# Cross attention on one Trainium2 core: row maxima by products in row tiles, other slots, and keys split by GpSimd

## The chip, the cores and the metric

One core of a Trainium2 chip runs the whole program in one launch. The metric is device time in microseconds. The engines are TensorE (PE in the rows, its weight loads PEld), VectorE (DVE), ScalarE (ACT), GpSimd (POOL) and SyncE (SP, which here issues all DMAs).

## The reference, cut to what matters

A decoder layer on x of 16 batches x 56 tokens x 128: token and channel attention, cross attention to 1500 context rows per batch, and a mixture of eight experts. The change lies in the cross attention, with 16 heads of depth 8:

```python
q = _split_heads(query @ wq.T + bq, B)      # 16, 16, 56, 8
k = _split_heads(value @ wk.T + bk, B)      # 16, 16, 1500, 8
v = _split_heads(value @ wv.T + bv, B)
scores = jnp.einsum('bhqd,bhkd->bhqk', q, k) / scale
attn = jax.nn.softmax(scores, axis=-1)
ctx = jnp.einsum('bhqk,bhkd->bhqd', attn, v)
```

## The kernel before

Three stages follow each other: the token and channel attention (to about 114 us), the cross attention (to about 523 us), and the experts. Each is a block with one instruction stream per engine; semaphores order them.

**Keys.** For each batch, `project_keys` (L203) makes the keys in three chunks of 500, head dimension on partitions, in PSUM. ScalarE reads each chunk twice in `read_keys` (L225): rounded to fp32r as `k_hi` (L234), then whole as `k_full` (L235), which frees the bank. GpSimd makes `k_lo` = `k_full` - `k_hi` in `split_keys` (L237, L244). Keys of batch 0 are made within the first stage (L412, L468, L735), those of batch 1 at the opening of the cross attention (L968, L1008, L1139), all others in the loop. Around both openings GpSimd also computes the reciprocal roots for a layer norm (L146, L148), VectorE applies them to eight tiles of 128 columns in `normed` (L122, L124), and in the first stage GpSimd then sets `values` to 1 (L413). SyncE copies `k_hi`, `k_lo` and `k_hi` again into `k_stack` (L918), so that one product of 97 rows gives the scores with their low parts and the negated maximum as a row.

**Maximum.** Before the scores of a batch, each query row's maximum is estimated from the high parts alone. The 896 rows (16 heads x 56 tokens) are seven tiles of 128. `q_block_hi` holds the queries of each row at the 8 partitions of its own head and zeros elsewhere (L973), so one product of 128 x 128 by 128 x 500 (`max_scores`, L1158 to L1172) gives a tile's scores for a chunk; 7 x 3 = 21 products per batch, each into a bank of its own. VectorE reduces each (`take_max`, L1072) into `chunk_max`, joins the chunks of tiles 0 to 3 and 4 to 6 (`join_max`, L1081); TensorE turns the result (`turn_max`, L1181), ScalarE negates it (L1018), and SyncE brings the rows to `q_stack` by seven DMAs (`load_shift`, L934).

**Order.** All engines walk through periods of one batch with 12 slots (KT), one per tile of 125 keys. A slot t begins with `scores` (L1183, four products of 97 rows, S below); ScalarE takes their exponentials (L1024). Four tiles at once are weighed with the values (`weigh`, L1201, 32 products of fp32, two passes each, W below) in WEIGH_SLOTS, on column tiles of 32. The sums are copied (L1030), the denominators made (L1220), inverted (L1094), the heads scaled (L1098) and projected (L1227, 56 columns) in the period after. Keys for batch b + 2, values for b + 1 and the two turns for b + 1 have slots of their own. MAX_PLACES says how many maximum products follow in each slot: right behind the scores, ahead of W, behind W. Those from slot EARLY on belong to batch b + 2, the others to b + 1. Key, value, output, turn and maximum results take the banks 4, 5 and 7 in turn (`bank_turns`); a use waits until the third use before it has been read (`take_bank`, L1153). Before the loop all 21 maxima of batch 0 and eight (AHEAD) of batch 1 are made.

Of the kernel before, what the change touches and what calls it, by code (L numbers as in the profile page):

```python
# [9 lines left out]
ALU = mybir.AluOpType  # L10
# [14 lines left out]
HALF = HQ // 2  # L25
# [55 lines left out]
def build(nc, x_in, ctx_in, mats_in, rows_in, cols_in, gate_in, consts_in, const_at, wgu_in, wd_in, out):  # L81
    ctx = ExitStack()
    with ctx:
# [85 lines left out]
        def later(n, first):  # L169
            return not isinstance(n, int) or n >= first  # L170
# [54 lines left out]
        def read_keys(act, b, j, u, c, bank=MISC):  # L225

            if later(b, 1):
                act.wait_ge(k_lo_ready, KC * (b - 1) + c + 1)
            act.wait_ge(k_projected, KC * b + c + 1)
            k = slice(KW * c, KW * c + KW)  # L230
            if c == 0 and later(b, 2):
                act.wait_ge(stack_loaded[j], 16 * STACK_DMAS * u)
                act.wait_ge(max_scored, QT7 * KC * (b - 1))
            nc.scalar.activation(k_hi[:, j, k], bank[:, 0:KW], ACT.Identity, bias=COL["bk"]).then_inc(k_hi_ready, 1)  # L234
            nc.scalar.activation(k_full[:, k], bank[:, 0:KW], ACT.Identity, bias=COL["bk"]).then_inc(k_ready, 1)  # L235

        def split_keys(pool, b, j, u):  # L237

            if later(b, 2):
                pool.wait_ge(stack_loaded[j], 16 * STACK_DMAS * u)  # L240
            for c in range(KC):
                pool.wait_ge(k_ready, KC * b + c + 1)
                k = slice(KW * c, KW * c + KW)
                nc.gpsimd.tensor_tensor(k_lo[:, j, k], k_full[:, k], k_hi[:, j, k].bitcast(F32), ALU.subtract  # L244
                                        ).then_inc(k_lo_ready, 1)
# [560 lines left out]
        with s2:  # L806


            EARLY = 8
            MAX_PLACES = [(2, 0, 2), (0, 0, 0), (1, 2, 0), (1, 0, 0), (0, 1, 0), (1, 0, 1),  # L810
                          (1, 0, 0), (1, 0, 0), (1, 0, 0), (2, 1, 1), (0, 0, 1), (0, 1, 1)]
            KEY_SLOTS, VALUE_SLOTS, TURN_SLOTS = [2, 3, 4], [1, 6, 7], [3, 8]
            SUMS_SLOT, DEN_SLOT, INVERT_SLOTS, SCALE_SLOT, OUT_SLOT = 1, 2, [3, 4], 4, 8
            RING, QUAD, WEIGH_SLOTS = 6, 4, [0, 5, 9]
            HALF_TILES = [slice(0, -(-HALF // 128)), slice(-(-HALF // 128), QT7)]
            HALF_ROWS = HALF_TILES[0].stop
            TURNING_BANKS = [4, 5, 7]
# [36 lines left out]
            def max_bank(b, n):  # L854
                return BANK_OF["max", n] if later(b, 1) else (n + 4) % 6
# [49 lines left out]
            with nc.Block() as block:  # L905

                @block.sync
                def _(sp):
# [21 lines left out]
                    def load_shift(b, j, a):  # L930

                        sp.wait_ge(rows_ready, 2 * b + a + 1)
                        for r, t in enumerate(range(HALF_TILES[a].start, HALF_TILES[a].stop)):
                            sp.dma_start(q_stack[SHIFT_ROW:SHIFT_ROW + 1, j, 128 * t:128 * t + 128].bitcast(F32),  # L934
                                         neg_rows[r:r + 1, j, a, :].bitcast(F32)).then_inc(shift_loaded[j], 16)
# [114 lines left out]
                def _(dve):  # L1050
# [18 lines left out]
                    def take_max(b, j, n):  # L1069

                        dve.wait_ge(max_scored, QT7 * KC * b + n + 1)
                        nc.vector.tensor_reduce(out=chunk_max[:, n // KC, n % KC:n % KC + 1],  # L1072
# [64 lines left out]
                def _(pe):  # L1137
# [20 lines left out]
                    def max_scores(b, j, n):  # L1158
# [3 lines left out]
                        if n < KC:  # L1162
                            pe.wait_ge(k_hi_ready, KC * b + n + 1)
# [4 lines left out]
                        elif n >= 6:  # L1168
                            pe.wait_ge(max_taken, n - 5)
                        t, c = n // KC, n % KC  # L1170
                        nc.tensor.matmul(PS[:, max_bank(b, n), 0:KW], q_block_hi[:, j, 128 * t:128 * t + 128],  # L1171
                                         k_hi[:, j, KW * c:KW * c + KW], start=True, stop=True).then_inc(max_scored, 1)  # L1172
# [449 lines left out]
```

## Time and profile before

| | us |
|---|---|
| three runs | 668.26, 673.27, 677.43; median 673.27 |
| profiled execution | 676.67, its span 674.9 |
| cross attention, from the scores of batch 1 to those of batch 14 | 173.44 to 478.29 of the span |
| mean granted clock of TensorE | 0.944 |

Times in the rows are microseconds from the span's start unless marked ns. An instruction's busy time runs from its start to its end; matmuls are pipelined, so the ends of one overlap with the starts of the next, and the distance from start to start tells what one costs the engine.

### The profile page before, as it was taken

What the parts mean: (1) busy time and instruction counts of PE and PEld (TensorE: products, weight loads), DVE (VectorE), ACT (ScalarE), POOL (GpSimd) and SP (SyncE); (2) the same over time, 40 slices, a digit from 0 to 9 for tenths busy, and PEclk for the clock granted to TensorE, in tenths of its full rate; (3) what the DMA queues carried; (4) which work ended last, traced back from release to release, by engine and by line L of the source; (5) the groups of instructions that cost most, each with busy time, mean ns of one, the idle gap of its engine ahead of it and who ended that gap; (6) DMA issues with size and microseconds to landing.
All of it is one profiled execution on the core that took longest, in us unless ns stands there. A gap on an engine that the chain in (4) does not pass through costs nothing. (4 is left out here: it accounts for less than half of the span.)

```text
span 674.9 us, 17191 instructions
## 1 busy us (share of the span) xinstructions
PE 601.8 (89%) x6538; PEld 488.5 (72%) x6538; DVE 449.3 (67%) x806; ACT 338.1 (50%) x522; POOL 179.1 (27%) x143
## 2 busy tenths in 40 slices
PE   3799376679999999999999999999987489999997
PEld 1566165337787778778777877877776379999997
DVE  5764775887777878787887787787822464444443
ACT  2467344207656756665675576566554253333321
POOL 2673601422322423232242324123000211121100
PEclk9799888669999999999999999999989589999999
DMA  5000001575745663674467366536620011111100
GB/s 207 1 2 2 0 1 37 114 157 106 177 111 121 137 156 94 137 160 121 107 137 168 99 141 139 131 97 139 133 100 2 10 50 48 47 47 47 47 17 29
DMA packets 26221, 60.33 MB, mean 89 GB/s; under 512 B 14408, under 2 KB 15304, under 8 KB 26184
## 3 DMA queue, kind: packets, MB, share of 16 engines
q1 hardware_dynamic: 26184, 59.82, 36.4%
q8 instruction: 25, 0.41, 0.3%
q14 instruction: 12, 0.10, 0.0%
HBM read 20.53 MB, written 0.46 MB: 31 GB/s over the span
## 5 line engine op out<-in xcount | busy, mean ns | idle before, releaser
L1072 DVE TENSOR_REDUCE chunk_max<-PS 128x1 f32<-128x500 f32 x336 | 214.2, 674 | 58.6 <-PE PS L1171 56.8
L1024 ACT ACTIVATE P<-PS 125x896 f32<-125x896 f32 x192 | 173.6, 914 | 122.2 <-PE PS L1195 121.3
L1171 PE MATMUL PS<-k_hi,q_block_hi 128*128 128x500 f32 x336 | 132.5, 449 | 8.2 <-ACT k_full L235 3.4
L1195 PE MATMUL PS<-q_stack,k_stack 97*125 97x224 f32 x768 | 122.2, 282 | 2.7 <-ACT P L1024 2.5
L1195 PEld LDWEIGHTS PS<-q_stack,k_stack 97*125 97x125 f32 x768 | 106.8, 190 | 17.9 <-issue 6.8
L1171 PEld LDWEIGHTS PS<-k_hi,q_block_hi 128*128 128x128 f32 x336 | 62.3, 197 | 39.9 <-ACT k_full L235 16.8
L244 POOL TENSOR_TENSOR k_lo<-k_full,k_hi 128x500 fp32r<-128x500 f32 x48 | 60.3, 1258 | 103.7 <-ACT k_full L235 103.7
L1513 DVE TENSOR_TENSOR hidden<-gated,PS 128x448 f32<-128x448 f32 x64 | 39.7, 621 | 70.0 <-PE PS L1570 63.6
L1211 PE MATMUL PS<-P,values 125*32 125x112 f32 x3072 | 85.2, 263 | 0.6 <-ACT P L1024 0.5
L1211 PEld LDWEIGHTS PS<-P,values 125*32 125x32 f32 x3072 | 73.3, 111 | 13.9 <-issue 10.4
L1425 ACT ACTIVATE gated<-PS 128x448 f32<-128x448 f32 x64 | 34.9, 546 | 81.3 <-PE PS L1570 76.7
L982 POOL TENSOR_TENSOR q_stack<-q_copies,consts 96x896 fp32r<-96x896 f32 x16 | 26.8, 1677 | 143.6 <-PE PS L1195 131.4
L1548 PEld LDWEIGHTS PS<-w_down,hidden 128*128 128x128 f32 x448 | 57.6, 191 | 1.5
L1548 PE MATMUL PS<-w_down,hidden 128*128 128x128 f32 x448 | 57.9, 274 | 0.0
L206 PE MATMUL PS<-ctxT,mats 128*128 128x500 f32 x96 | 48.7, 589 | 7.1 <-ACT k_full L235 5.5
L1568 PE MATMUL PS<-T_hi,w_hi 128*128 128x448 f32 x128 | 52.5, 410 | 1.8 <-DVE hidden L1513 1.8
L214 PE MATMUL PS<-mats,ctxT 128*125 128x128 f32 x384 | 49.7, 273 | 0.0
L214 PEld LDWEIGHTS PS<-mats,ctxT 128*125 128x125 f32 x384 | 48.0, 188 | 1.3 <-issue 0.2
L1570 PE MATMUL PS<-T_hi,w_lo 128*128 128x448 f32 x128 | 47.7, 373 | 0.0
L1569 PE MATMUL PS<-T_lo,w_hi 128*128 128x448 f32 x128 | 47.7, 373 | 0.0
L234 ACT ACTIVATE k_hi<-PS,cols 128x500 fp32r<-128x500 f32 x48 | 32.3, 672 | 24.5 <-PE PS L206 23.2
L1390 POOL TENSOR_TENSOR w_lo<-w_gate_up,w_hi 128x1024 fp32r<-128x1024 f32 x8 | 19.0, 2376 | 92.2 <-ACT w_hi L1409 92.2
(139 smaller groups left out, 698.1 us busy)
## 6 DMA issues: line engine op xcount, KB each, us to landing
k_stack<-k_hi SPq DMA_DIRECT2D x128, 187.5 KB, 4.6
ctxT<-ctx_in SPq DMA_DIRECT2D x16, 750.0 KB, 4.3
k_stack<-k_lo SPq DMA_DIRECT2D x64, 187.5 KB, 4.5
w_gate_up<-wgu_in SPq DMA_DIRECT2D x8, 512.0 KB, 4.1
w_down<-wd_in SPq DMA_DIRECT2D x8, 256.0 KB, 2.8
q_stack<-neg_rows SPq DMA_DIRECT2D x112, 0.5 KB, 1.9
q_copies<-q_hi SPq DMA_DIRECT2D x8, 112.0 KB, 2.6
mats<-mats_in SPq DMA_DIRECT2D x1, 832.0 KB, 5.5
```

The source lines that it names most:

```text
L206: nc.tensor.matmul(bank[:, 0:KW], MAT["wk"], ctxT[:, j, KW * c:KW * c + KW], start=True, stop=True).then_inc(k_projected, 1)
L214: last = nc.tensor.matmul(bank[0:KR, 128 * t:128 * t + 128], ctxT[:, j, k0:k0 + KR], MAT["wv"], start=True, stop=True)
L244: nc.gpsimd.tensor_tensor(k_lo[:, j, k], k_full[:, k], k_hi[:, j, k].bitcast(F32), ALU.subtract).then_inc(k_lo_ready, 1)
L1024: nc.scalar.activation(P[:, t % RING, :].rearrange("p (a n) -> p a n", a=2), PS[0:KR, 2 * (t % 2):2 * (t % 2) + 2, 0:HALF], ACT.Exp).then_ ...
L1072: nc.vector.tensor_reduce(out=chunk_max[:, n // KC, n % KC:n % KC + 1], in_=PS[:, max_bank(b, n), 0:KW], axis=AX.X, op=ALU.max).then_inc(m ...
L1171: nc.tensor.matmul(PS[:, max_bank(b, n), 0:KW], q_block_hi[:, j, 128 * t:128 * t + 128], k_hi[:, j, KW * c:KW * c + KW], start=True, stop= ...
L1195: last = nc.tensor.matmul(PS[0:KR, 2 * (t % 2) + g // 2, o:o + GH * N], k_stack[:, j, g, KR * t:KR * t + KR], q_stack[0:SHIFT_ROW + 1, j, ...
L1211: last = nc.tensor.matmul(PS[32 * k:32 * k + 32, 6, 2 * N * r:2 * N * r + 2 * N], values[:, j, t, g, :], P[:, t % RING, 2 * N * g:2 * N * ...
L1548: last = nc.tensor.matmul(PS[:, 4 + 2 * j + p // 4, 128 * (p % 4):128 * (p % 4) + 128], hidden[:, j, t, 128 * p:128 * p + 128], w_down[:, ...
L1568: nc.tensor.matmul(bank, w_hi[:, j, w], hi, start=True, stop=False)
L1569: nc.tensor.matmul(bank, w_hi[:, j, w], lo, start=False, stop=False)
L1570: nc.tensor.matmul(bank, w_lo[:, j, w], hi, start=False, stop=True).then_inc(done, 1)
```

## The change

1. Each of the seven row tiles of queries touches only certain heads, so its product reads only the partitions (TILE_ROWS) where `q_block_hi` isn't zero: 32 rows for tiles 0, 2, 4 and 6, each in another quarter of the array, 64 for tiles 1 and 5, all 128 for tile 3. The results are the same sums. The order is by place (TILE_ORDER) and, within the groups of places, by chunk (MAX_ORDER): four products of 32 rows for each chunk, then two of 64 for each chunk, then three full ones. A chunk of keys is first waited for at products 0, 4 and 8.
2. EARLY, MAX_PLACES and all slots are new; three products per chunk group may follow each other in one place.
3. ScalarE reads a chunk of keys once, into `k_full`. GpSimd multiplies it by 1 into `k_hi` (fp32r, rounded), waits for that, and subtracts as before. The wait on `max_scored` moves to GpSimd.

```diff
--- before.py
+++ after.py
@@ -228,19 +228,19 @@
                 act.wait_ge(k_lo_ready, KC * (b - 1) + c + 1)
             act.wait_ge(k_projected, KC * b + c + 1)
             k = slice(KW * c, KW * c + KW)
-            if c == 0 and later(b, 2):
-                act.wait_ge(stack_loaded[j], 16 * STACK_DMAS * u)
-                act.wait_ge(max_scored, QT7 * KC * (b - 1))
-            nc.scalar.activation(k_hi[:, j, k], bank[:, 0:KW], ACT.Identity, bias=COL["bk"]).then_inc(k_hi_ready, 1)
             nc.scalar.activation(k_full[:, k], bank[:, 0:KW], ACT.Identity, bias=COL["bk"]).then_inc(k_ready, 1)
 
         def split_keys(pool, b, j, u):
 
             if later(b, 2):
                 pool.wait_ge(stack_loaded[j], 16 * STACK_DMAS * u)
+                pool.wait_ge(max_scored, QT7 * KC * (b - 1))
             for c in range(KC):
                 pool.wait_ge(k_ready, KC * b + c + 1)
                 k = slice(KW * c, KW * c + KW)
+                nc.gpsimd.tensor_tensor(k_hi[:, j, k], k_full[:, k], C["ones"][:, 0:1].broadcast_to([128, KW]), ALU.mult
+                                        ).then_inc(k_hi_ready, 1)
+                pool.wait_ge(k_hi_ready, KC * b + c + 1)
                 nc.gpsimd.tensor_tensor(k_lo[:, j, k], k_full[:, k], k_hi[:, j, k].bitcast(F32), ALU.subtract
                                         ).then_inc(k_lo_ready, 1)
 
@@ -806,14 +806,19 @@
         with s2:
 
 
-            EARLY = 8
-            MAX_PLACES = [(2, 0, 2), (0, 0, 0), (1, 2, 0), (1, 0, 0), (0, 1, 0), (1, 0, 1),
-                          (1, 0, 0), (1, 0, 0), (1, 0, 0), (2, 1, 1), (0, 0, 1), (0, 1, 1)]
-            KEY_SLOTS, VALUE_SLOTS, TURN_SLOTS = [2, 3, 4], [1, 6, 7], [3, 8]
-            SUMS_SLOT, DEN_SLOT, INVERT_SLOTS, SCALE_SLOT, OUT_SLOT = 1, 2, [3, 4], 4, 8
-            RING, QUAD, WEIGH_SLOTS = 6, 4, [0, 5, 9]
-            HALF_TILES = [slice(0, -(-HALF // 128)), slice(-(-HALF // 128), QT7)]
+            EARLY = 9
+            MAX_PLACES = [(1, 0, 3), (0, 0, 0), (0, 0, 0), (0, 0, 2), (0, 0, 0), (0, 2, 2), (0, 1, 0), (0, 1, 0), (1, 0, 0), (1, 0, 0), (2, 1, 2), (2, 0, 0)]
+            KEY_SLOTS, VALUE_SLOTS, TURN_SLOTS = [2, 4, 6], [2, 5, 8], [4, 9]
+            SUMS_SLOT, DEN_SLOT, INVERT_SLOTS, SCALE_SLOT, OUT_SLOT = 0, 1, [1, 4], 6, 9
+            RING, QUAD, WEIGH_SLOTS = 6, 4, [0, 5, 10]
+            TILE_ROWS = [(0, 32), (0, 64), (32, 64), (0, 128), (64, 96), (64, 128), (96, 128)]
+            TILE_ORDER = [0, 2, 4, 6, 1, 5, 3]
+            HALF_TILES = [slice(0, 4), slice(4, 7)]
             HALF_ROWS = HALF_TILES[0].stop
+            MAX_ORDER = ([(place, c) for c in range(KC) for place in range(0, 4)]
+                         + [(place, c) for c in range(KC) for place in range(4, 6)]
+                         + [(6, c) for c in range(KC)])
+            FIRST_OF_CHUNK = {MAX_ORDER.index((0, c)): c for c in range(KC)}
             TURNING_BANKS = [4, 5, 7]
             assert sum(map(sum, MAX_PLACES)) == QT7 * KC
             AHEAD = sum(map(sum, MAX_PLACES[EARLY:]))
@@ -930,7 +935,7 @@
                     def load_shift(b, j, a):
 
                         sp.wait_ge(rows_ready, 2 * b + a + 1)
-                        for r, t in enumerate(range(HALF_TILES[a].start, HALF_TILES[a].stop)):
+                        for r, t in enumerate(TILE_ORDER[HALF_TILES[a]]):
                             sp.dma_start(q_stack[SHIFT_ROW:SHIFT_ROW + 1, j, 128 * t:128 * t + 128].bitcast(F32),
                                          neg_rows[r:r + 1, j, a, :].bitcast(F32)).then_inc(shift_loaded[j], 16)
 
@@ -1069,7 +1074,7 @@
                     def take_max(b, j, n):
 
                         dve.wait_ge(max_scored, QT7 * KC * b + n + 1)
-                        nc.vector.tensor_reduce(out=chunk_max[:, n // KC, n % KC:n % KC + 1],
+                        nc.vector.tensor_reduce(out=chunk_max[:, MAX_ORDER[n][0], MAX_ORDER[n][1]:MAX_ORDER[n][1] + 1],
                                                 in_=PS[:, max_bank(b, n), 0:KW], axis=AX.X, op=ALU.max
                                                 ).then_inc(max_taken, 1)
 
@@ -1159,17 +1164,19 @@
 
                         if n == 0:
                             pe.wait_ge(q_blocks, b + 1)
-                        if n < KC:
-                            pe.wait_ge(k_hi_ready, KC * b + n + 1)
+                        if n in FIRST_OF_CHUNK:
+                            pe.wait_ge(k_hi_ready, KC * b + FIRST_OF_CHUNK[n] + 1)
                         if later(b, 1):
                             take_bank(max_bank(b, n), (max_taken, QT7 * KC * b + n + 1))
                         elif n == 4:
                             pe.wait_ge(q_split, 2)
                         elif n >= 6:
                             pe.wait_ge(max_taken, n - 5)
-                        t, c = n // KC, n % KC
-                        nc.tensor.matmul(PS[:, max_bank(b, n), 0:KW], q_block_hi[:, j, 128 * t:128 * t + 128],
-                                         k_hi[:, j, KW * c:KW * c + KW], start=True, stop=True).then_inc(max_scored, 1)
+                        place, c = MAX_ORDER[n]
+                        t = TILE_ORDER[place]
+                        r = slice(*TILE_ROWS[t])
+                        nc.tensor.matmul(PS[:, max_bank(b, n), 0:KW], q_block_hi[r, j, 128 * t:128 * t + 128],
+                                         k_hi[r, j, KW * c:KW * c + KW], start=True, stop=True).then_inc(max_scored, 1)
 
                     def turn_max(b, a):
 
```

## Rows read from the trace of the kernel before

The timeline views have: start, us busy, engine, line, operation, output<-inputs, shapes, count, and in brackets the idle time before and what ended it.

**Rows 1.** Windows view, 13 periods: length, busy of PE, PEld, DVE, ACT, POOL, granted clock.

```profile
173.44:478.29 304.85, 301.81 (x3939) 242.07 (x3940) 244.49 (x391) 193.06 (x274) 92.17 (x66) 1.00 0.56 129
```

**Rows 2.** Timeline of VectorE in one period.

```profile
312.70 3.78 DVE L1072 TENSOR_REDUCE chunk_max<-PS 128x1 f32<-128x500 f32 x6 [0.70 <-PE PS L1171]
```

**Rows 3.** Timeline of TensorE, parts of one period.

```profile
309.72 0.85 PE L1171 MATMUL PS<-k_hi,q_block_hi 128*128 128x500 f32 x3
310.50 1.74 PE L1211 MATMUL PS<-P,values 125*32 125x112 f32 x64
312.17 0.49 PE L1171 MATMUL PS<-k_hi,q_block_hi 128*128 128x500 f32 x1
312.50 0.59 PE L1195 MATMUL PS<-q_stack,k_stack 97*125 97x224 f32 x4
312.93 0.40 PE L1171 MATMUL PS<-k_hi,q_block_hi 128*128 128x500 f32 x1
313.17 0.59 PE L1195 MATMUL PS<-q_stack,k_stack 97*125 97x224 f32 x4
313.60 0.63 PE L1171 MATMUL PS<-k_hi,q_block_hi 128*128 128x500 f32 x2
314.25 0.69 PE L1195 MATMUL PS<-q_stack,k_stack 97*125 97x224 f32 x4
...
321.21 0.59 PE L1195 MATMUL PS<-q_stack,k_stack 97*125 97x224 f32 x4
322.06 0.50 PE L1171 MATMUL PS<-k_hi,q_block_hi 128*128 128x500 f32 x1 [0.24 <-ACT k_full L235]
322.39 1.00 PE L206 MATMUL PS<-ctxT,mats 128*128 128x500 f32 x2
323.23 0.27 PE L1181 MATMUL PS<-consts,max_turn 128*128 128x128 f32 x1
...
323.77 1.01 PE L206 MATMUL PS<-ctxT,mats 128*128 128x500 f32 x2
324.73 0.49 PE L1171 MATMUL PS<-k_hi,q_block_hi 128*128 128x500 f32 x1
```

**Rows 4.** Timeline of the token attention: products on row and column tiles.

```profile
54.04 0.23 PEld L665 LDWEIGHTS PS<-q_block,qkT 32*64 32x64 f32 x16 [0.17 <-issue]
54.04 0.64 PE L665 MATMUL PS<-q_block,qkT 32*64 32x224 f32 x16
```

**Rows 5.** Groups by line and shape, GpSimd, whole span (count | busy us, mean ns).

```profile
L244 POOL TENSOR_TENSOR k_lo<-k_full,k_hi 128x500 fp32r<-128x500 f32 x48 | 60.3, 1258 | 103.7 <-ACT k_full L235 103.7
L973 POOL TENSOR_TENSOR q_block_hi<-q_hi,consts 128x896 fp32r<-128x896 f32 x16 | 27.0, 1687 | 4.3 <-DVE q_all L1066 4.3
L387 POOL TENSOR_TENSOR q_square<-squared,consts 128x224 f32<-128x224 f32 x16 | 9.1, 593 | 5.5 <-DVE scaled L519 5.5
```

**Rows 6.** Line L1098, the scaling: ns of one, min/median/max.

```profile
L1098 DVE TENSOR_TENSOR heads_out<-heads_out,heads_sum x16: 392/1479/1485, 184.0 to 521.1; 128x224 f32<-128x224 f32 x16
```

**Rows 7.** SyncE's timeline, and the page's DMA issues (median us to landing last).

```profile
309.78 1.78 SPq L934 DMA_DIRECT2D q_stack<-neg_rows  x3
...
q_stack<-neg_rows SPq DMA_DIRECT2D x112, 0.5 KB, 1.9
```

**Rows 8.** First stage, 74 to 86 us: line L124, who waited, and GpSimd's timeline.

```profile
L124 DVE TENSOR_SCALAR Y<-Z,moments,rstd x8: 330/806/6415, 75.2 to 84.8; 128x128 f32<-128x128 f32 x8
...
  PE PS L635: 7.6, 2
...
75.40 2.45 POOL L244 TENSOR_TENSOR k_lo<-k_full,k_hi 128x500 fp32r<-128x500 f32 x2
...
79.49 5.21 POOL L413 MEMSET values<- 125x6144 f32 x1
```

**Rows 9.** Opening of the cross attention: GpSimd's and VectorE's timelines.

```profile
118.62 2.44 POOL L244 TENSOR_TENSOR k_lo<-k_full,k_hi 128x500 fp32r<-128x500 f32 x2
118.70 4.91 DVE L124 TENSOR_SCALAR q_all<-X,moments,rstd 128x128 f32<-128x128 f32 x8 [2.05 <-POOL rstd L148]
```

## The prediction, made before the change was run

> **What bounds the kernel now.** I read the windows view of the cross attention first. From the second batch's scores to the fifteenth's lie 13 periods in 304.85 us, 23.45 us each; TensorE is busy for 99% of it at full granted clock, VectorE for 80%, ScalarE for 63%, GpSimd for 30% [rows 1]. So TensorE sets the period. Its timeline, read start to start (its busy times overlap), shows what a period is made of [rows 3]: four score products (S) take 0.43 us (312.50 to 312.93), or about 0.51 behind fp32 work (turn and S together 0.54, 323.23 to 323.77); a maximum product takes 0.23 to 0.24; weighing (W) takes 1.67; a key projection 0.84. Three places aren't work. S at 321.21 is followed by a maximum only at 322.06, 0.85 later instead of 0.43, on a bank that ScalarE must empty of keys. The key projection at 323.77 lasts 0.96 instead of 0.84 for the same reason. The two products at 313.60 last 0.65 instead of 0.47. VectorE needs 3.78 / 6 = 0.63 us per maximum in a run [rows 2], 13.2 us of the period for 21.
>
> The end of the chain of waits lies in the last stage, which the change doesn't touch, so I go by stages: the period times about 14, and the serial openings in which keys 0 and 1 are made.
>
> **1. Maximum products in row tiles.** Of 21 per batch, 12 now read 32 rows, 6 read 64, and 3 all 128. By the new slots they come in these groups: slot 0 one, then (behind W) three; slot 3 two; slot 5 two, W, two; slots 6, 7, 8 one full product each; slot 9 one; slot 10 three, W, two; slot 11 two. That is 9 groups for 18 tiled products.
> What a group gains: the token attention already runs 32-row tiles. 16 fp32 products of L665, 32 rows by 64 columns each, take 0.64 us together, where one by one 16 times the 0.11 us that 224 elements take in S would be 1.7; their 16 weight loads take 0.23 us together, 0.014 each, against 0.11 in S [rows 3, 4]. So loads and products of different row groups run side by side, and a group of two or three costs about what one costs, 0.24 us. Removed: 18 - 9 = 9 times 0.23, less 0.01 for each extra start: 2.0 us per period. If row tiles ran one by one, it would be 0.
> What a group costs: a change of the array's shape. W is the model, 32 columns wide. Three products ahead of W take 0.78 us, so the last takes 0.78 - 2 x 0.235 = 0.31, 0.08 more than its like; the first behind W takes 0.33 (312.17 to 312.50), 0.10 more, since its weights could not be loaded ahead [rows 3]. A change costs 0.08 + 0.10 = 0.18 to 0.19 us. W and the output projection are changes already. New are: S to 1 product and group to S in slot 0 (2), slot 3 (2), slot 5 (2), S to group in slot 9 (1), slot 10 (2), slot 11 (2), 11 in all, 11 x 0.19 = 2.1 us. Bounds: 0 (everything hidden) and 0.33 each (3.6 us), a whole product behind a change. I take 0.19, the row nearest. So tiling by itself gives 2.0 - 2.1 = 0.1 us lost per period, no gain.
>
> **2. Keys read once, and the slots.** ScalarE loses one of two reads of 0.65 us per chunk, so a key bank is free 0.65 us sooner, and the slots put a value projection or a turn behind each key projection (key slots 2, 4, 6). The waits on it go: 0.42 (at 321.21) + 0.12 (at 323.77) + 2 x 0.10 for weights not loaded ahead [rows 3] = 0.73 us. The wait of slot 0 at 313.60, 0.18 us, was for ScalarE after three S in short succession; now W lies between slots 10 and 11, and it goes too. What is late next is VectorE: slots 10, 11 and 0 now have 11 maxima (before, the 11 were spread over slots 9 to 0). 11 x 0.63 = 6.9 us of VectorE against 7.3 us of TensorE by the same rows, with three banks. By hand: product 7 needs the bank of product 4, taken 3.85 us after slot 10 begins, when TensorE could go on at 3.7. I charge 0.25 us per period; the bounds are 0 and 1.0 (three groups broken by a bank wait, 0.33 each, a full product behind a change).
> Scaling of the heads takes 0.39 us alone and 1.48 while GpSimd's split runs [rows 6]. In slot 6 it falls between the splits of chunks 1 and 2, about 0.5 us clear. That frees 1.1 us of VectorE, not of TensorE: nothing off the sum, 0.4 us back if it collides.
> The second turn is a slot later. In [rows 7] its three DMAs are issued from 309.78 for 1.78 us, and slot 0 began at 314.25 [rows 3], 4.5 us after the first issue. Now slots 10 and 11 alone lie between turn and slot 0: S, three products, W, two (3.1 us), S, two (1.1), which leaves 3.6 us from the first issue. Needed are two issues of 0.59 and 1.9 to landing, 3.1 [rows 7]. Hidden with 0.5 us to spare; what it is late beyond that goes on the path in full, and I keep 0 to 0.4 us for it within the bounds of the waits above.
> GpSimd: three multiplications per batch. Of this form the trace has 224 elements at 0.59 us and 896 at 1.69; between them 500 is 1.03 (bounds 0.59 and 1.69) [rows 5]. With waits 3.4 us per period on an engine idle for 16. Chunk 0 is wanted in slot 9, made in slot 3; chunk 2 is read in slot 6 and wanted in slot 0; the low part of chunk 2 is done by slot 8 and waited for in slot 11. Nothing on the path.
> Period: -2.0 + 2.1 - 0.73 - 0.18 + 0.25 = -0.6 us, about 22.9. Times 14: -8 us.
>
> **3. The openings.** Here the extra GpSimd work isn't hidden. VectorE's normalisation of Y, eight instructions, lasts from 75.2 to 85.1 (the last starts at 84.8 and takes 0.33), beside the three splits (two from 75.40) and the memset of the values (79.49, 5.21 us); one of the eight takes 0.33 alone and 6.4 at worst [rows 8]. TensorE waits 7.6 us for it [rows 8]. I read this as a port that the two share by turns: one instruction of VectorE passes at each end of a GpSimd instruction. Now six GpSimd instructions stand ahead of the memset: 3 x (1.03 + 0.1 wait + 1.25 + 0.07) = 7.4 us from 75.40, so the memset begins at 82.8 and ends at 88.0. Seven of VectorE's eight have passed by then, the eighth comes behind the memset: 88.3 instead of 85.1, +3.2 us. Bounds: +4.6 with 1.69 per multiplication, -2.0 if all eight pass before the memset.
> The Trainium skill, "SBUF — State Buffer", section "Who interferes with whom", says that a two-port VectorE instruction and a GpSimd one exclude each other for a whole instruction, by order of issue; by that rule the sum is this one or the -2.0, depending on whether VectorE gets in twice at a pause of GpSimd.
> The same at the opening of the cross attention: VectorE's eight instructions last 4.91 us from 118.70, beside splits that begin at 118.62 [rows 9]. Six GpSimd instructions end at 118.62 + 3 x 2.36 = 125.7, the sixth of the eight passes there, the last is done at 126.5 instead of 123.6: +2.9 us (2.2 to 3.9). Queries, blocks and the first maxima follow serially. The 29 maxima before the loop are VectorE's, 0.63 each, as before. Together +6.1 us.
>
> **Sum.** 676.67 (the profiled execution) - 8.4 + 6.1 = 674.4 us. It lies 0.5% above the median of the three, 673.27, so I forecast 674.4 x 673.27 / 676.67 = 671 us. A measurement here tells about 2%, 13.5 us, from no change: this is inside.
>
> **Rivals.**
> A. *Changes of shape are free beside row tiles* (weights of another row group can load under a running product). Then 2.1 us per period goes: 14 x 2.1 = 29 us, 642 us. For it: loads side by side in [rows 4]. Against: 0.10 us behind every W [rows 3]. A half of it (only the load is hidden, 0.10 of 0.19) gives 656. The Trainium skill, "TensorEngine Tiling (Array Packing)", section "Key Properties", says that a change of mode, not of tile, drains the array, while its table gives up to 4x for 32 rows; by the first nothing is gained in groups of two, by the second the gain is that of this rival. Chance 0.14 with the half.
> B. *VectorE's maxima become the bound (slower).* Place: slots 10 to 0, three banks for 11 maxima; every product that waits for its bank breaks its group and pays 0.33 alone. It decides once VectorE is more than about 0.4 us behind TensorE at slot 10. Price: 1.0 to 1.5 us per period, so the period is 23.9 to 24.4; 671 + 14 x 1.2 = 688. For it: nine groups of which each needs two or three of three banks at once. Against: VectorE has 60.4 / 13 = 4.6 us idle per period [rows 1], and scaling gets shorter. Chance 0.13.
> C. *Row tiles don't overlap at this shape* (128 columns, 500 elements, fp32r): the 2.0 us stay, 671 + 28 = 699. [rows 4] show tiles of 64 columns only. Chance 0.05.
> D. *VectorE slips through at GpSimd's pauses*: the first opening gives back 5.2 us: 666. Chance 0.2; it is in the range of the likeliest.
>
> **How the numbers follow.** The likeliest (with D) has 0.68: 671, its own range 662 to 681 from 0 to 1.0 us of bank waits, the two openings and 0.1 us more or less per period. Range for 8 in 10: 653 (half of A) to 689 (B). Faster by over 2% (below 660): A, and a tenth of the likeliest: 0.21. Slower by over 2% (above 687): B above its middle, C, and a little of the likeliest: 0.17. Within 2%: 0.62.
>
> **What would show it.** Period near 22.9 us; starts within a group about 0.01 us apart; the last S before a group 0.09 us longer to the next start, and the first S behind it 0.1; no wait of TensorE on the keys' read; multiplications near 1.03 us; Y's normalisation ended near 88.3 and that of the cross attention near 126.5; scaling at 0.39 us. Wrong if a group of three takes over 0.5 us, if the period is above 23.5 or below 22, or if the first maximum of the cross attention isn't about 6 us later than before.

## The result and the profile after

The changed kernel took 681.4 us (median of 4, 679.55 to 683.67), the kernel before, on the same chip and between these runs, 675.35 (668.26 to 679.19): ratio 1.0158, interval 1.0099 to 1.0218. The ratio is larger than that of the medians because it leaves out executions of before that lie far above its fastest. The change is slower, by about 1.6%; the interval begins clear of 1 and reaches just past 2%. The profiled execution took 682.42 us, its span is 680.4 and its mean granted clock 0.921 (before: 0.944).

Where the time went, by sections that begin and end at the same work in both kernels (columns as in [rows 1]: start, end and length, then busy time of PE, PEld, DVE, ACT, POOL with counts, granted clock, DMA share, GB/s). The windows view of the changed kernel:

```profile
0.00:71.52 71.52, 52.43 (x690) 34.29 (x690) 43.23 (x102) 36.70 (x64) 36.26 (x49) 1.00 0.14 50
71.52:83.96 12.44, 1.61 (x6) 0.72 (x4) 12.44 (x9) 1.88 (x2) 12.05 (x8) 0.62 0.00 0
83.96:119.38 35.42, 26.21 (x165) 22.47 (x166) 21.24 (x40) 14.39 (x43) 3.22 (x4) 0.80 0.10 22
119.38:154.83 35.45, 21.24 (x45) 9.46 (x43) 30.21 (x45) 2.38 (x5) 14.90 (x11) 0.54 0.59 124
154.83:179.64 24.81, 23.48 (x230) 17.51 (x230) 15.80 (x27) 12.93 (x17) 7.78 (x7) 0.83 0.44 100
```

And that of the kernel before:

```profile
0.00:75.20 75.20, 55.99 (x688) 36.70 (x688) 43.34 (x101) 37.73 (x66) 36.24 (x49) 0.93 0.13 48
75.20:85.10 9.90, 1.76 (x6) 0.72 (x6) 9.89 (x9) 2.96 (x4) 9.12 (x5) 0.75 0.00 0
85.10:118.70 33.60, 23.98 (x164) 20.32 (x164) 21.14 (x40) 14.87 (x44) 3.22 (x4) 0.87 0.10 23
118.70:151.57 32.87, 22.48 (x45) 11.15 (x46) 27.61 (x45) 3.67 (x8) 11.93 (x8) 0.64 0.62 132
151.57:173.44 21.87, 20.84 (x231) 15.96 (x229) 16.01 (x27) 14.06 (x20) 4.24 (x4) 0.99 0.49 116
```

Line by line: the work up to the normalisation of Y isn't touched by the change and was 3.7 us shorter at a higher granted clock (1.00 against 0.93); that is luck of this pair of executions. The normalisation of Y: +2.5. The section behind it, not touched either: +1.8, at 0.80 against 0.87. The opening of the cross attention: +2.6. Its first period: +2.9, with the granted clock at 0.83 instead of 0.99. From the second batch's scores to the fifteenth's the changed kernel takes 485.88 - 179.64 = 306.24 us against 304.85 [rows 1], +1.4; and from there to the end 194.5 against 196.6, -2.1. The sum is +5.5. The pieces that the change touches (the two openings, the first period, the thirteen) make +9.4; I had forecast -2.3 for them. The first maximum product of the cross attention starts at 132.5 us instead of 129.3; without the two untouched sections (-3.7 and +1.8) that is the 5.1 us of the openings.

The thirteen periods of the changed kernel aren't alike. Start to start of slot 0, by the windows and the scores' timeline: 24.39, 23.16, 24.38, 23.17, 24.43, 23.16, 24.37, 23.20, 24.38, 23.15, 22.82, 22.85, 22.78. Three of them in the windows view, under them slot 0 alone in the first two, and the slow stretch within the first:

```profile
179.64:204.04 24.40, 24.40 (x304) 19.11 (x304) 17.17 (x30) 12.77 (x18) 9.56 (x9) 0.93 0.55 128
204.04:227.20 23.16, 22.85 (x304) 17.70 (x304) 18.00 (x32) 13.54 (x19) 10.52 (x9) 1.00 0.58 135
417.43:440.25 22.82, 22.82 (x303) 17.70 (x303) 17.42 (x30) 12.83 (x19) 9.80 (x9) 1.00 0.58 135
...
179.64:184.33 4.69, 4.69 (x72) 3.78 (x72) 1.37 (x3) 1.16 (x2) 2.39 (x2) 0.64 1.00 228
204.04:207.18 3.14, 3.14 (x74) 2.38 (x73) 1.87 (x4) 1.61 (x3) 2.97 (x2) 1.00 0.80 187
...
180.30:183.71 3.41, 3.41 (x62) 2.98 (x65) 0.71 (x2) 0.92 (x1) 1.73 (x2) 0.50 0.93 226
```

At full clock and without a gap a period takes 22.82 us: the 22.9 forecast. In every second period of the first ten the clock was granted at half (1.2 instead of 2.4 GHz) for a stretch that began 0.7 to 1.5 us behind the start of slot 0, and slot 0 took 4.69 instead of 3.14 us, 1.55 more. The other five of these ten end with a gap of 0.3 us on TensorE (busy 22.85 of 23.16), so four of the five slow stretches come right behind such a gap. TensorE's timeline shows it, at the end of the sixth period:

```profile
317.61 0.68 PE L1202 MATMUL PS<-q_stack,k_stack 97*125 97x224 f32 x4
318.22 0.49 PE L1178 MATMUL PS<-k_hi,q_block_hi 32*128 32x500 f32 x3
318.64 1.74 PE L1218 MATMUL PS<-P,values 125*32 125x112 f32 x64
320.31 0.49 PE L1178 MATMUL PS<-k_hi,q_block_hi 32*128 32x500 f32 x2
320.73 0.69 PE L1202 MATMUL PS<-q_stack,k_stack 97*125 97x224 f32 x4
321.36 0.69 PE L1178 MATMUL PS<-k_hi,q_block_hi 32*128 32x500 f32 x2
322.34 0.69 PE L1202 MATMUL PS<-q_stack,k_stack 97*125 97x224 f32 x4 [0.29 <-issue]
```

Three row-tiled maximum products (318.22) take 0.42 us to the next start, two (320.31) also 0.42: one product of 0.23 and one change of shape of 0.19, however many tiles. The last line is slot 0 of the next period: `issue` says that TensorE waited for nothing but its own instruction stream. The loop holds two batches, and the gap stands at its five turns (ahead of batches 3, 5, 7, 9 and 11) and not where the loop has ended (ahead of 13). The first of the thirteen, ahead of batch 1, has another wait in that place, and the maxima wait a little for VectorE (lines of the timeline and of the waits view: total us, times, longest):

```profile
179.64 0.69 PE L1202 MATMUL PS<-q_stack,k_stack 97*125 97x224 f32 x4 [0.53 <-DMA q_stack<-neg_rows]
...
PEld PS L1178 <- DVE chunk_max L1077: 3.0, 13, 0.2
```

The openings, in VectorE's and GpSimd's timelines:

```profile
71.52 12.44 DVE L124 TENSOR_SCALAR Y<-Z,moments,rstd 128x128 f32<-128x128 f32 x8 [2.04 <-POOL rstd L148]
...
119.38 7.44 DVE L124 TENSOR_SCALAR q_all<-X,moments,rstd 128x128 f32<-128x128 f32 x8 [2.05 <-POOL rstd L148]
...
71.70 1.04 POOL L241 TENSOR_TENSOR k_hi<-k_full,consts 128x500 fp32r<-128x500 f32 x1
72.82 1.24 POOL L244 TENSOR_TENSOR k_lo<-k_full,k_hi 128x500 fp32r<-128x500 f32 x1
...
78.59 5.22 POOL L413 MEMSET values<- 125x6144 f32 x1
```

Against [rows 8, 9] the first lasts 12.44 instead of 9.9 us and the second 7.44 instead of 4.91; the multiplication takes 1.04. Over the span, groups by line (page) and the scaling's durations:

```profile
L241 POOL TENSOR_TENSOR k_hi<-k_full,consts 128x500 fp32r<-128x500 f32 x48 | 49.0, 1022 | 121.2 <-ACT k_full L231 121.2
...
L1103 DVE TENSOR_TENSOR heads_out<-heads_out,heads_sum x16: 379/382/392, 195.1 to 528.3; 128x224 f32<-128x224 f32 x16
```

The scaling, 1479 ns in [rows 6], is at 382: it now misses GpSimd's splits.

### The profile page after: what moved, and what is told of

It is laid out like the page before. It is cut to its first block and busy times, and to the rows that moved or that the text cites. A ratio compares the mean times of both kernels' runs of the same rounds, so it can differ in the third digit from the quotient of the medians.

```text
span 680.4 us, 17179 instructions
## 1 busy us (share of the span) xinstructions
PE 603.9 (89%) x6538; PEld 481.5 (71%) x6538; DVE 438.1 (64%) x806; ACT 310.7 (46%) x474; POOL 228.2 (34%) x191
## 5 line engine op out<-in xcount | busy, mean ns | idle before, releaser
L1077 DVE TENSOR_REDUCE chunk_max<-PS 128x1 f32<-128x500 f32 x336 | 210.6, 672 | 61.1 <-PE PS L1178 58.4
L1202 PE MATMUL PS<-q_stack,k_stack 97*125 97x224 f32 x768 | 131.6, 295 | 5.0 <-DMA q_stack<-neg_rows 2.3
L1202 PEld LDWEIGHTS PS<-q_stack,k_stack 97*125 97x125 f32 x768 | 104.5, 192 | 34.3 <-issue 29.2
L1178 PE MATMUL PS<-k_hi,q_block_hi 32*128 32x500 f32 (+2 forms) x336 | 106.9, 529 | 6.6 <-DVE q_all L1071 2.6
L1218 PE MATMUL PS<-P,values 125*32 125x112 f32 x3072 | 91.4, 275 | 0.0
L241 POOL TENSOR_TENSOR k_hi<-k_full,consts 128x500 fp32r<-128x500 f32 x48 | 49.0, 1022 | 121.2 <-ACT k_full L231 121.2
L1218 PEld LDWEIGHTS PS<-P,values 125*32 125x32 f32 x3072 | 79.0, 117 | 11.1 <-issue 8.3
L1178 PEld LDWEIGHTS PS<-k_hi,q_block_hi 32*128 32x128 f32 (+2 forms) x336 | 42.5, 196 | 37.3 <-issue 12.9
L252 DVE TENSOR_TENSOR values<-PS,rows 125x512 f32<-125x512 f32 x48 | 33.0, 690 | 22.6 <-PE PS L214 22.6
```

Of the source, the lines that this page charges most:

```text
L241: nc.gpsimd.tensor_tensor(k_hi[:, j, k], k_full[:, k], C["ones"][:, 0:1].broadcast_to([128, KW]), ALU.mult).then_inc(k_hi_ready, 1)
L1077: nc.vector.tensor_reduce(out=chunk_max[:, MAX_ORDER[n][0], MAX_ORDER[n][1]:MAX_ORDER[n][1] + 1], in_=PS[:, max_bank(b, n), 0:KW], axis=AX ...
L1178: nc.tensor.matmul(PS[:, max_bank(b, n), 0:KW], q_block_hi[r, j, 128 * t:128 * t + 128], k_hi[r, j, KW * c:KW * c + KW], start=True, stop= ...
L1202: last = nc.tensor.matmul(PS[0:KR, 2 * (t % 2) + g // 2, o:o + GH * N], k_stack[:, j, g, KR * t:KR * t + KR], q_stack[0:SHIFT_ROW + 1, j, ...
L1218: last = nc.tensor.matmul(PS[32 * k:32 * k + 32, 6, 2 * N * r:2 * N * r + 2 * N], values[:, j, t, g, :], P[:, t % RING, 2 * N * g:2 * N * ...
```

## The experiments

Three theories. **T**: the row tiles lower the granted clock. **W**: it falls because TensorE pauses, for a bank or at the turn of the loop. **S**: the tiles' overlap is worth more than their changes cost, so that full rows would be slower still. "Before" is run beside each; all ratios are to it. (The expectation below counts six stretches at half clock; five lie in the thirteen periods, the sixth at 508 us.)

**Full rows.** All of the change but the tiles:

```diff
-                        r = slice(*TILE_ROWS[t])
+                        r = slice(0, 128)
```

> The changed kernel, but every maximum product reads all 128 rows (no row tiles); slots, order and keys as changed. Theory T (row tiles): 9 more product times of 0.23 us and 11 fewer changes of shape at 0.19 us, so TensorE's time per period stays about 22.8 us, and the half-rate stretches of the changed kernel in the loop (six of 3.4 us, 1.55 us each) are due to the row tiles and are gone: some 672 us, 1 to 1.5% below the changed kernel, all periods 22.7 to 23.2. Rival W (waits): the clock falls because TensorE pauses for a bank and at the turn of the loop around slots 11 and 0; then the same stretches appear with full rows too and the time stays near 681. Rival S (overlap is worth more than the changes cost): the period is above 23.4 and the time above 683.

673.17 us, ratio 0.996 (0.9925 to 0.9994). Windows of the opening's first period and two of the loop:

```profile
156.73:178.04 21.31, 20.62 (x231) 16.45 (x229) 15.54 (x27) 12.61 (x17) 7.40 (x7) 0.97 0.51 119
178.04:200.88 22.84, 22.84 (x303) 18.64 (x304) 17.28 (x30) 12.85 (x19) 9.86 (x9) 1.00 0.58 137
200.88:224.15 23.27, 22.98 (x305) 18.65 (x304) 17.93 (x32) 13.57 (x19) 10.58 (x9) 1.00 0.59 135
```

Same order, banks and gap, and no stretch at half clock in any of the thirteen, which take 298.97 us instead of 306.24. At full clock its periods, 22.84 and 23.27, are those of the changed kernel: the tiles as used are worth 0.1 us or less (forecast: 0.1 lost), and they bring the fall of the clock. It isn't one profile only: the mean granted clock of all ten executions was 0.935 to 0.947, that of the changed kernel's eight 0.921 to 0.928. S falls, and W as far as pauses alone would do it; whether the tiles need the pause beside them, the kernels with no gap below answer.

**Tiles in the two groups of three only.**

```diff
-                        r = slice(*TILE_ROWS[t])
+                        r = slice(*TILE_ROWS[t]) if n in (1, 2, 3, 9, 10, 11) else slice(0, 128)
```

> The changed kernel with row tiles only for the two groups of three (products 1 to 3 ahead of W in slot 10, and 9 to 11 behind W in slot 0); all others read 128 rows. By the prices of theory T (0.23 us a product, 0.19 a change, W being a change anyway) each group of three saves 2 x 0.23 and pays one change: 2 x (0.46 - 0.19) = 0.5 us per period less than with full rows, so the period is 22.2 to 22.4 us, without half-rate stretches in the loop: about 665 us. If the clock falls as in the changed kernel, about 673. If changes of shape cost more than 0.23 each, no better than full rows.

667.42 us, ratio 0.9913 (0.9879 to 0.9947). Windows, first period and one of the loop:

```profile
156.38:178.38 22.00, 20.47 (x231) 15.90 (x229) 16.34 (x28) 12.76 (x17) 8.18 (x7) 0.97 0.52 120
178.38:200.72 22.34, 22.34 (x304) 18.05 (x304) 16.55 (x29) 12.70 (x18) 9.09 (x9) 1.00 0.58 136
```

The two groups save 22.84 - 22.34 = 0.50 us. By the prices of the prediction: four products at 0.23 less two new changes at 0.19, 0.54. No half clock in the loop.

**Keys read twice by ScalarE again** (new slots and tiles kept), and **keys read once alone** (slots and tiles of before):

```diff
+            nc.scalar.activation(k_hi[:, j, k], bank[:, 0:KW], ACT.Identity, bias=COL["bk"]).then_inc(k_hi_ready, 1)
             nc.scalar.activation(k_full[:, k], bank[:, 0:KW], ACT.Identity, bias=COL["bk"]).then_inc(k_ready, 1)
...
-                nc.gpsimd.tensor_tensor(k_hi[:, j, k], k_full[:, k], C["ones"][:, 0:1].broadcast_to([128, KW]), ALU.mult
-                                        ).then_inc(k_hi_ready, 1)
```

The second kernel is the reverse of this diff, put into the kernel before.

> The changed kernel with ScalarE reading each chunk of keys twice and GpSimd only subtracting, as before (part 3 undone); row tiles and slots as changed. Theory P (shared port): the two openings give back 2.5 us each, 5 us; in the loop a key bank is free 0.67 us later, which the slots cover, and the period stays 22.8 (24.4 with a half-rate stretch): about 676 us. Rival: the keys' path doesn't matter in the openings (TensorE or the clock decides), and it stays at 681; or the later bank opens waits of 0.3 us and more per period, and it is above 683.

> The kernel before with the keys read once by ScalarE and split by GpSimd (part 3 alone; old slots, full rows). Theory P: the openings cost 2.5 us each; in the loop the waits on the keys' read shrink by up to 0.65 us each (0.3 to 0.7 us per period, 14 periods: 4 to 9 us): 670 to 676 us, equal to before within 1%. Scaling (slot 4) meets the longer GpSimd work and stays at 1.48 us or more. Rival: nothing is gained in the loop, then 680 us.

Read twice: 676.59 us, ratio 1.0025 (0.9976 to 1.0074). Read once alone: 672.96, ratio 0.9976 (0.9933 to 1.0018). A period of the first kernel in the windows view:

```profile
169.95:193.45 23.50, 23.49 (x304) 18.08 (x304) 16.85 (x29) 14.45 (x21) 6.19 (x6) 1.00 0.52 129
```

Two of the second:

```profile
179.09:201.96 22.87, 22.87 (x304) 18.57 (x304) 17.68 (x31) 12.97 (x19) 9.91 (x9) 1.00 0.58 137
201.96:224.99 23.03, 22.93 (x304) 18.65 (x304) 18.07 (x31) 13.46 (x19) 10.34 (x9) 1.00 0.58 136
```

The first kernel has all tiles, the slots and the 0.3 us gaps of the changed one, and yet only one of its thirteen periods (25.05 us, at 0.93) has a stretch at half clock. Reading once is worth 23.50 - 22.82 = 0.68 us with the new slots, and 23.45 - 22.95 = 0.5 with the old. For the first kernel I had expected 22.8: wrong, since I had given the gain to the slots. The slots alone are worth nothing (22.84 and 23.27 of the full rows against 22.87 and 23.03: if anything 0.1 us lost per period, at the turn of the loop).

**Neighbours on the same rows**: the row tiles stay, but products that follow each other read the same 32 rows.

```diff
-            MAX_ORDER = ([(place, c) for c in range(KC) for place in range(0, 4)]
-                         + [(place, c) for c in range(KC) for place in range(4, 6)]
-                         + [(6, c) for c in range(KC)])
+            MAX_ORDER = [(place, c) for place in range(QT7) for c in range(KC)]
```

> The changed kernel with the maximum products in another order: all chunks of one row tile behind each other, so that most neighbours in a group (7 of the 9 extra products) read the same rows and can't run side by side; shapes, changes of shape, slots and sums stay. Theory T (row groups run side by side, which is worth 0.23 us per extra product): a group of two takes 0.23 us more, a group of three on the same rows 0.46; the period grows by 7 x 0.23 = 1.6 us to 24.4 at full clock, the time by 22 us to some 700, or less by the half-rate stretches that go (the period's length has changed). Rival: starts 0.01 us apart don't mean side by side (VectorE paces), and the time stays near 681.

694.99 us, ratio 1.0361 (1.0306 to 1.0417). A full-clock period, one that isn't, and a group of three in TensorE's timeline with the start behind it:

```profile
332.58:356.75 24.17, 24.17 (x304) 18.36 (x304) 17.71 (x31) 12.99 (x19) 9.98 (x9) 1.00 0.55 127
303.39:332.58 29.19, 29.11 (x304) 22.14 (x304) 18.07 (x31) 13.52 (x19) 10.28 (x9) 0.82 0.45 105
...
335.29 0.94 PE L1176 MATMUL PS<-k_hi,q_block_hi 32*128 32x500 f32 x3
336.16 0.59 PE L1200 MATMUL PS<-q_stack,k_stack 97*125 97x224 f32 x3
```

Three products on the same rows take 0.87 us to the next start, three on different rows 0.42. So the overlap is real, and rival C is out; the 1.35 us per period is what seven of the nine overlapped products are worth in this kernel. The clock fell in two of the thirteen periods (29.19 and 25.75 us), each time 1.5 us behind the start of slot 0 and with no gap of TensorE above 0.1 us ahead of it: the tiles bring the fall without the pause.

**Tiles in the old slots**: the kernel before with TILE_ROWS, TILE_ORDER and MAX_ORDER of the change, nothing else.

> The kernel before with row tiles and their order alone; keys by ScalarE and the slots as before. The old places cut the 18 tiled products into 12 groups, with 19 or so new changes of shape. Theory T: 6 x 0.23 = 1.4 us saved and 19 x 0.19 = 3.6 us paid, +2.2 us per period, 25.7 us: about 706 us, more if the clock falls at times. Rival (a change costs only what a group wins): 675.

712.62 us, ratio 1.0577 (1.0486 to 1.0667). Windows of two periods:

```profile
180.04:205.02 24.98, 24.90 (x305) 18.22 (x303) 18.05 (x30) 15.03 (x22) 7.18 (x6) 1.00 0.54 125
205.02:231.59 26.57, 26.50 (x306) 19.54 (x304) 18.06 (x30) 15.02 (x22) 7.16 (x6) 0.94 0.50 118
```

Where tiled products stand mostly singly or in pairs, tiles cost 1.5 us per period at full clock (24.98 against 23.45; expected 2.2): more changes of shape, and less overlap to pay for them. And stretches at half clock again, in five of the thirteen periods, each about 1.6 dear, again 0.7 to 1.5 us behind the start of slot 0, and with no gap of 0.1 us or more in the loop. With other slots and keys read twice, this is a second schedule in which the clock falls once the products are tiled.

**Products 6, 7, 8 on full rows**, those of slot 11 and the one ahead of W in slot 0, just where the stretches began:

```diff
-                        r = slice(*TILE_ROWS[t])
+                        r = slice(*TILE_ROWS[t]) if n not in (6, 7, 8) else slice(0, 128)
```

> The changed kernel with products 6, 7 and 8 alone on all 128 rows: they lie in slots 11 and 0, just ahead of where each half-rate stretch began. Prices of T: three changes less (0.57), one product's time more (0.23): the period is 22.5 at full clock. If the fall of the clock hangs on the load of TensorE in just this stretch, no half-rate stretch is left in the loop and the time is about 668. If it hangs on the row tiles wherever they are, or on where the period stands against something with its own beat, some stretches remain (1.5 us each), in other places: 668 to 676.

673.62 us, ratio 1.0036 (1.0002 to 1.007). Windows, first period and one of the loop:

```profile
156.68:181.59 24.91, 23.91 (x231) 17.61 (x229) 16.42 (x28) 12.94 (x17) 8.14 (x7) 0.83 0.46 106
181.59:204.17 22.58, 22.58 (x303) 17.57 (x304) 16.75 (x29) 12.73 (x18) 9.17 (x9) 1.00 0.57 134
```

No half clock in the loop; but the first period, tiled elsewhere as in the changed kernel, still has it (0.83). That the place of these tiles decides in the loop is suggested, not shown: there are also three tiled products fewer, the period is 0.24 us shorter, and it is one profiled execution (the others' mean clock was 0.889 to 0.937).

**The changed kernel once more**, to see whether the stretches stay where they are.

> The changed kernel unchanged, a second time. If the half-rate stretches belong to it, the profile shows again some five in the loop, each 0.7 to 1.6 us behind the beginning of a slot 0, periods of 22.8 or 23.2 us without one and 24.4 with one, and about 681 us. If they were an accident of one execution, another number in other places, and a time of 672 to 681.

681.1 us, ratio 1.0128 (1.0058 to 1.0197). Windows of three periods:

```profile
179.71:207.29 27.58, 27.58 (x303) 21.25 (x303) 16.99 (x29) 12.97 (x18) 9.38 (x9) 0.81 0.47 111
230.48:253.29 22.81, 22.81 (x304) 17.70 (x304) 17.39 (x30) 12.79 (x19) 9.79 (x9) 1.00 0.59 135
369.91:394.31 24.40, 24.40 (x304) 18.95 (x304) 17.42 (x30) 12.81 (x19) 9.80 (x9) 0.93 0.55 126
```

They move: a long one in the first of the thirteen, then three of 24.4 us in the seventh, ninth and eleventh, and 22.8 or 23.15 in the others. All lie again in periods whose slot 0 stands behind a gap. The total is the same within 0.3 us.

**The openings**: ScalarE reads the keys of batches 0 and 1 twice, as before, and GpSimd splits only. First in the changed kernel, then in the one with tiles in the groups of three, then in that one with full rows for the maxima of batches 0 and 1 as well.

```diff
+        def opening(b):
+            return isinstance(b, int) and b < 2
...
+            if opening(b):
+                nc.scalar.activation(k_hi[:, j, k], bank[:, 0:KW], ACT.Identity, bias=COL["bk"]).then_inc(k_hi_ready, 1)
...
-                nc.gpsimd.tensor_tensor(k_hi[:, j, k], ...
+                if not opening(b):
+                    nc.gpsimd.tensor_tensor(k_hi[:, j, k], ...
```

> The changed kernel with the keys of batches 0 and 1 alone read twice by ScalarE as before; from batch 2 on everything as changed. Theory P: the normalisation in the first opening takes 9.8 us instead of 12.4, in the second 4.5 instead of 7.4: 5 us off, 676 us, if the half-rate stretches stay. They may stand elsewhere, since all starts are earlier: 670 to 678. Rival: the openings are not on the path: 681.

> The kernel with row tiles only in the two groups of three, and the keys of batches 0 and 1 (the two openings) read twice by ScalarE as before; from batch 2 on by GpSimd. Theory P (the longer GpSimd work holds VectorE's normalisation by the shared port in both openings, 2.5 us each): 5 us below the kernel with the threes alone (667.4): 662 us, period 22.3. Rival: another wait takes over in the openings: 665 to 667.

> The kernel with the threes in row tiles and the first two batches' keys by ScalarE (663.7 us), and in addition all maximum products of batches 0 and 1 on 128 rows. Theory T says that row tiles in the opening also keep the clock low: up to 31 us at half rate there and 24.9 us for the first period, against 17 and 10 us and 21.3 with full rows. Then the first period falls to 21.3 to 22.5 and the time to 661. Rival: the opening is VectorE's and the clock there has other causes: 663 to 664, first period above 24.

In the changed kernel: 672.98 us (663.88 to 677.44), ratio 0.9983 (0.9936 to 1.003), some 8 us under the changed kernel (681.1 on the same chip), more than the 5 us of the openings. The profiled execution is one of its two slowest (677.25 us): its normalisations took 9.89 and 4.91 us, as before, and the first and the eleventh of the thirteen had a stretch at half clock (27.59 and 24.42 us). The faster ones weren't profiled, so what the other 3 us are is open. With groups of three: 663.73, ratio 0.9864 (0.9779 to 0.9948). VectorE's timeline of it:

```profile
75.02 9.72 DVE L124 TENSOR_SCALAR Y<-Z,moments,rstd 128x128 f32<-128x128 f32 x8 [2.04 <-POOL rstd L148]
...
120.83 3.99 DVE L124 TENSOR_SCALAR q_all<-X,moments,rstd 128x128 f32<-128x128 f32 x8 [2.05 <-POOL rstd L148]
```

9.72 and 3.99 us instead of 12.44 and 7.44: both openings are back. But its first period took 24.91 us at 0.82. With full rows in batches 0 and 1: **661.31 us** (653.8 to 663.9), ratio 0.9794 (0.9711 to 0.9876), the fastest of all and faster than both kernels. Its windows, first period and one of the loop:

```profile
152.52:174.39 21.87, 20.67 (x231) 16.32 (x229) 16.37 (x28) 12.77 (x17) 8.21 (x7) 0.95 0.53 120
174.39:196.75 22.36, 22.36 (x304) 18.05 (x304) 16.57 (x29) 12.71 (x18) 9.08 (x9) 1.00 0.55 136
```

The first period is 21.87 us again. That alone doesn't prove T for the opening, since the first kernel with groups of three had a first period of 22.00 us with the very tiles of this 24.91, and the intervals of the last two kernels overlap (0.9779 to 0.9948 and 0.9711 to 0.9876). But over 118 to 165 us of the span, the opening and the start of the first period, the granted clock was 0.69 to 0.75 in the five profiles with full rows there and 0.56 to 0.67 in the nine with tiles.

**Keys read once from batch 2 on, in the kernel before** (its slots, full rows).

> The kernel before (old slots, full rows) with keys by GpSimd from batch 2 on and by ScalarE twice for batches 0 and 1. Keys alone had periods of 22.9 us and 673 us; theory P gives back 5 us in the openings: 667 to 668. If new slots are worth nothing by themselves, this equals full rows in new slots less the same 5 us. Rival: as keys alone, 672 to 673.

667.84 us, ratio 0.988 (0.9829 to 0.9931). Timelines of GpSimd and VectorE in its first opening:

```profile
74.96 2.46 POOL L250 TENSOR_TENSOR k_lo<-k_full,k_hi 128x500 fp32r<-128x500 f32 x2
78.47 1.30 POOL L250 TENSOR_TENSOR k_lo<-k_full,k_hi 128x500 fp32r<-128x500 f32 x1 [1.05 <-ACT k_full L236]
79.72 5.30 POOL L419 MEMSET values<- 125x6144 f32 x1
...
74.78 5.08 DVE L124 TENSOR_SCALAR Y<-Z,moments,rstd 128x128 f32<-128x128 f32 x8 [2.04 <-POOL rstd L148]
```

GpSimd paused for 1.05 us ahead of the third split, all eight of VectorE's instructions got through before the memset, and the normalisation took 5.08 us instead of 9.9. That is what rival D describes, seen in a kernel with three GpSimd instructions ahead of the memset instead of six. It fits the spread of before's own runs (668 to 679), but that this is its cause is argued, not shown.

## Why the prediction was wrong

I forecast 671 us in a range of 653 to 689 and "within 2%". The time, 681.4, lies in both, but the sign was wrong: -2.3 us became a significant loss. By the steps:

- **The failing step** is in the first sentence on what bounds the kernel: TensorE busy "at full granted clock" [rows 1]. That was a property of the kernel before, and I carried it over as a constant into every term. It cost 5 x 1.55 = 7.8 us in the loop and about 2.9 in the first period (3.5 against the 21.31 us of the full rows): 10.7, of which nothing was in the sum, in the rivals or in the range. Without it the pieces that the change touches come to 9.4 - 10.7 = -1.3 us, against -2.3 forecast. None of my rivals was this one; the time that the rival of VectorE's banks gave (688) has another mechanism, which the full-rows kernel, with the same banks, shows absent.
- **Tiles**, -2.0 + 2.1: right. 22.84 with full rows, 22.82 with tiles. Both halves are real: the overlap (0.42 instead of 0.87 for three) and the price of a change (0.42 less the 0.23 of a product; in the old slots the changes outweigh the overlap by 1.5 us). Rival A is out: had changes been free, the period would be 22.9 - 2.1 = 20.8. The Trainium skill, "TensorEngine Tiling (Array Packing)", section "Key Properties", says that a change of mode drains the engine; the 0.42 us of a group of two agree.
- **Waits on the keys and slots**, -0.73 - 0.18 + 0.25 = -0.66: the size is right (0.68 with the new slots), the owner wrong. I gave it to "keys read once, and the slots"; it belongs to the single read. The new slots are worth nothing by themselves. The bank wait, priced at 0.25, is there: 0.2 us in each of the thirteen.
- **Turn of the loop**: missing from the sum. TensorE is idle for 0.3 us at every second slot 0, and the period ahead of it is 0.35 longer (before: 0.1), 5 x 0.35 = 1.8 us in the loop. With 22.82 as the base: 13 x 22.82 = 296.7, plus 7.8, plus 1.8, is the 306.2 measured.
- **The openings**, +3.2 and +2.9: +2.5 and +2.6. Right in mechanism, 1 us too dear together. One VectorE instruction passing at each end of a GpSimd one gave the times. The Trainium skill, "SBUF — State Buffer", section "Who interferes with whom", has the exclusion for a whole instruction, which the rows bear out; the alternation is what these rows add. Rival D didn't come true in the changed kernel; the last experiment's 5.08 us show that such a slip happens.
- **GpSimd's multiplication**, 1.03: 1.02. **Scaling**, 0.39: 0.38. **The turn's rows** landed 0.9 to 1.3 us ahead of slot 0 (forecast 0.5) in eleven of the thirteen and 0.4 ahead in one: hidden. Ahead of the first of them TensorE waited 0.53 us for them, which nothing in the sum has (before: 0.2).

What stays open: why tiles lower the clock, and why it falls where it does. Shown is that it falls in the loop in all six profiles with all 18 tiles (17.1, 20.5, 13.7, 3.4, 13.7 and 17.1 us at half clock in the thirteen periods: the changed kernel, the same again, with the old openings, with keys read twice, same rows, old slots), and in none of the eight with full rows, with six tiles or with fifteen; that each stretch begins within 1.6 us of the start of a slot 0; and that they move between executions of one kernel. In the changed kernel they began 47.8 us apart and two periods take 47.55, so that each began 0.2 us later in its slot 0 than the one before (0.7 to 1.5), and behind the fifth there was none: that the clock's falls keep a time of their own, against which the period has to lie badly, is suggested by it, not shown. That keys read twice left one stretch of five points the same way.

## What to carry to other kernels

A granted clock of 1.00 in the profile of before came here with its mix of products on TensorE, and is not a given: where a change makes the products smaller or narrower, put a rival "half clock for a stretch" beside the sum, priced from rows at either level. Tile rows where three or more products of different row groups follow each other, and leave pairs and single products whole: a group cost one product and a change of shape here, so pairs gained nothing. And work moved to an idle GpSimd was only free where VectorE wasn't in a serial stretch beside it; here two batches of sixteen were worth an exception of 5 us.

## What was unexpected of the hardware

- The clock fell to half while TensorE's busy time was 24.40 of 24.40 us. The Trainium skill, "TensorE: Matmul & The Clock Gate", section "HAM oscillation — how this bites in real kernels", tells of falls behind gaps in the engine's work. Ahead of the falls in the changed kernel stand gaps too, but of 0.3 us (the first 0.53); the kernel with full rows has the same gaps of 0.3 and no fall, and two tiled kernels fall with no gap above 0.1 us. The measurement decides: here neither gaps nor the busy share foretold the clock.
- The turn of a loop cost TensorE 0.3 us in this order of instructions and 0.1 in the other, with the same amount of work.
- Half the clock for 3.4 us cost 1.55 us: slot 0 took 4.69 instead of 3.14 us, since the stretch covers only a part of it (granted 0.64 over the slot).
- The memset of the values, which reads nothing, held VectorE's normalisation like the splits did: the last of the eight instructions, 0.33 us alone, was done with the memset's end, at 83.95 us. Where a pause of 1.05 us let all eight through before it, they took 5.08 us.
